# Output projection of an attention layer: single-precision matmuls replaced by three terms of halves, for all batches but the last

## The reference, cut to what matters

```python
    x = L0_attn_x
    xn = _layernorm(x, axis=-1)
    x = x + _L0_attn_ref(xn, ...) + _L0_ffn_ref(xn, ...)

    # the end of _L0_attn_ref, which the change is about
    y = jnp.einsum('bhqk,bhkd->bhqd', att, v)
    y = y.transpose(0, 2, 1, 3).reshape(Bx, Sx, Dx)
    return y @ W_proj + b_proj
```

## Time and profile before

| | us |
|---|---|
| median of three runs | 3735.48 |
| lowest and highest of them | 3733.85, 3745.34 |
| the profiled execution, its own time | 3740.65 |
| its span, first to last instruction | 3738.8 |
| TensorE (matmul) busy | 3660.0 (98%) |
| VectorE busy | 2638.5 (71%) |
| ScalarE busy | 1199.3 (32%) |
| GpSimd busy | 930.6 (25%) |

### The profile page before, as it was taken

One profiled execution on the slowest core, in us unless ns is written; L12 is line 12 of the kernel. 1 busy time (PEld: TensorE's weight loads), 2 busy tenths in 40 slices (PEclk: granted clock), 3 DMA queues, 4 the chain that ended last, 5 costly groups with the idle time before them and its releaser, 6 DMA issues.

```text
span 3738.8 us, 63849 instructions
## 1 busy us (share of the span) xinstructions
PE 3660.0 (98%) x21836; PEld 2699.9 (72%) x21836; DVE 2638.5 (71%) x3834; ACT 1199.3 (32%) x2313; POOL 930.6 (25%) x462
## 2 busy tenths in 40 slices
PE   8999999999999999999999999999999999999999
PEld 6657657657656566566565578888888888888887
DVE  6675766766766766766766667777777777777776
ACT  2542532533523524514414412222222222222222
POOL 0560741642632724615615500000000000000000
PEclk9999999999999999999999999999999999999999
DMA  6525435335336245254256331100111110011110
GB/s 199 124 72 178 109 101 175 77 123 165 80 120 173 63 144 155 58 185 123 73 179 172 119 122 34 34 31 28 34 34 34 34 32 31 30 34 34 34 34 28
DMA packets 180526, 337.02 MB, mean 90 GB/s; under 512 B 42688, under 2 KB 50368, under 8 KB 179392
## 3 DMA queue, kind: packets, MB, share of 16 engines
q1 hardware_dynamic: 156096, 280.47, 26.5%
q10 hardware_dynamic: 24192, 53.49, 4.2%
HBM read 213.92 MB, written 118.43 MB: 89 GB/s over the span
## 4 chain that ended last, share of the span: by engine, by line
PE 90%; issue 2%; DMA 2%; DVE 2%; POOL 2%; ACT 1%; SPq 0%; ACTq 0%; DVEq 0%; POOLq 0%
PE f_ps L1523 26%; PE ps_dense L1016 13%; PE f_ps_o L1535 13%; PE ps_st L1072 9%; PE ps_s L1041 5%; PE ps_y L1093 4%; PE ps_dense L1180 4%; PE ps_dense L1093 3%; PE ps_dense L1111 3%; PE ps_dense L1041 2%; PE f_ps L1515 1%; PE ps_st L1079 1%; DMA stack<-mr 1%; POOL stage L585 1%; PE ps_s L1046 1%
## 5 line engine op out<-in xcount | busy, mean ns | idle before, releaser
L1523 PE MATMUL f_ps<-wgu,xqt 128*128 128x512 f32 (+1 forms) x4608 | 992.9, 373 | 1.4 <-DVE xqt L1383 1.4
L1523 PEld LDWEIGHTS f_ps<-wgu,xqt 128*128 128x128 f32 x4608 | 842.4, 188 | 123.0 <-DVE xqt L1383 1.7
L933 ACT ACTIVATE pt<-ps_st 128x512 f32<-128x512 f32 (+3 forms) x1152 | 550.4, 526 | 540.4 <-PE ps_st L1072 354.8
L653 DVE TENSOR_REDUCE mx<-ps_s 128x1 f32<-128x640 f32 (+3 forms) x512 | 523.8, 1023 | 212.2 <-PE ps_s L1046 203.1
L585 POOL TENSOR_TENSOR stage<-stage,pt 128x1536 f32<-128x1536 f32 (+2 forms) x176 | 519.1, 2950 | 15.2
L1535 PE MATMUL f_ps_o<-wd,hqt 128*128 128x512 f32 x2112 | 513.4, 396 | 0.2 <-DVE hqt L1409 0.2
L583 POOL TENSOR_TENSOR stage<-pt 128x1792 f32<-128x1792 f32 x64 | 256.5, 4009 | 882.6 <-ACT pt L933 882.6
L1535 PEld LDWEIGHTS f_ps_o<-wd,hqt 128*128 128x128 f32 x2112 | 392.6, 189 | 79.5 <-DVE hqt L1409 0.6
L1016 PE MATMUL ps_dense<-arena,wa 128*128 128x512 f32 x1536 | 384.1, 399 | 11.1 <-DVE rob L701 6.2
L1016 PEld LDWEIGHTS ps_dense<-arena,wa 128*128 128x128 f32 x1536 | 281.1, 189 | 73.7 <-issue 10.8
L653 DVE TENSOR_REDUCE mx<-ps_dense 128x1 f32<-128x128 f32 (+3 forms) x424 | 204.4, 482 | 87.5 <-PE ps_dense L1046 78.1
(11 more groups left out here) (135 smaller groups left out, 4943.1 us busy)
## 6 DMA issues: line engine op xcount, KB each, us to landing
qk_scratch<-stage SPq DMA_DIRECT2D x128, 512.0 KB, 2.8
stack<-qk_scratch SPq DMA_DIRECT2D x192, 256.0 KB
arena<-qk_scratch SPq DMA_DIRECT2D x192, 256.0 KB
xs<-in_L_attn_x SPq DMA_DIRECT2D x64, 256.0 KB, 3.6
rob<-in_L_attn_x ACTq DMA_DIRECT2D x64, 256.0 KB, 2.8
acc_scratch<-rob ACTq DMA_DIRECT2D x64, 256.0 KB, 2.2
xt<-in_L_attn_x SPq DMA_DIRECT2D x64, 256.0 KB, 2.6
at<-acc_scratch SPq DMA_DIRECT2D x64, 256.0 KB, 2.6
```

The source lines that it names most:

```text
L653: nc.vector.tensor_reduce(mx[:, h * ST + q:h * ST + q + 1], scores_bank(p, n)[:, 0:(q + 1) * P], axis=AX.X, op=ALU.max, negate=True).then_ ...
L933: nc.scalar.activation(exps(kt)[:, h, q - kt * P:q - kt * P + n], ps_st[:, w % ST_RING, 0:n], ACT.Exp, scale=SCALE).then_inc(st_exp, 1)
L1523: last = nc.tensor.matmul(ps[:, SLOT[c], gu, 0:n].rearrange("p (j n) -> p j n", n=P), xqt[:, a, k], wgu[:, b, gu * FC + f // P:gu * FC + ( ...
```

## The change

For all batches but the last (`not final`) the output projection is made as the first stage is, in three terms of halves. The high half of `wp` is made by ScalarE and its low half by GpSimd, two pieces each, behind pair 5, in the place of stack 0, for each batch anew. The high half of `yt` is made by ScalarE in the place of stack 1 and its low half by GpSimd in place over `yt`: groups 0 and 1 behind pair 6, group 2 behind pair 7. Group 3 of tiles 0 and 1 stays whole; for the other six tiles ScalarE makes its high halves in two pieces (256 and 512 columns) and VectorE the low ones, between `low_of_x(0)` and `low_of_x(1)`. The fourth `high_of_x` comes behind them on ScalarE. Four semaphores are new.

```diff
+    yt_low = memory.over("yt_low", [P, G, S], F32R, "yt")
...
+    wp_halves = stack01[:, 0].rearrange("p a (c n) -> p (a c) n", n=D)
+    yt_high = stack01[:, 1]
+    WHOLE = 2
+    LAST_COLS = [slice((ST // 2 + WHOLE) * P, S), slice(0, S // 2)]
+    NHALVES = G - 1 + len(LAST_COLS)
...
+            def low_of_wp(i):
+                rows = slice(i * KC // 2, (i + 1) * KC // 2)
+                pool.wait_ge(p_hi, ONE + b * 2 + i + 1)
+                nc.gpsimd.tensor_tensor(wp_halves[:, KC + i * KC // 2:KC + (i + 1) * KC // 2], wp[:, rows],
+                                        wp_halves[:, rows].bitcast(F32), ALU.subtract).then_inc(p_lo, 1)
+
+            def low_of_y(g):
+                pool.wait_ge(y_hi, ONE + b * NHALVES + g + 1)
+                nc.gpsimd.tensor_tensor(yt_low[:, g], yt[:, g], yt_high[:, g].bitcast(F32),
+                                        ALU.subtract).then_inc(y_lo, 1)
...
                 for kt in SUM_ORDER[:summed(p)]:
                     sum_up(p, kt)
+                if not final and p == PAIRS - 3:
+                    for i in range(2):
+                        low_of_wp(i)
+                if not final and p == PAIRS - 2:
+                    for g in range(G - 2):
+                        low_of_y(g)
+                if not final and p == PAIRS - 1:
+                    low_of_y(G - 2)
...
             divide(PAIRS - 1)
             if not final:
-                for t in range(XR):
+                low_of_x(b + 1, 0)
+                for i, cols in enumerate(LAST_COLS):
+                    dve.wait_ge(y_hi, ONE + b * NHALVES + G + i)
+                    dve.wait_ge(y_lo, ONE + b * NHALVES + G - 1 + i)
+                    nc.vector.tensor_tensor(yt_low[:, G - 1, cols], yt[:, G - 1, cols],
+                                            yt_high[:, G - 1, cols].bitcast(F32), ALU.subtract).then_inc(y_lo, 1)
+                for t in range(1, XR):
                     low_of_x(b + 1, t)
...
+            def high_of_wp(i):
+                rows = slice(i * KC // 2, (i + 1) * KC // 2)
+                nc.scalar.activation(wp_halves[:, rows], wp[:, rows], ACT.Copy).then_inc(p_hi, 1)
+
+            def high_of_y(g):
+                act.wait_ge(y_div, ONE + b * PAIRS * 2 + (g + 1) * 4)
+                nc.scalar.activation(yt_high[:, g], yt[:, g], ACT.Copy).then_inc(y_hi, 1)
...
+                    if not final and p == PAIRS - 3 and kt >= ST - 3 and kt < ST - 1:
+                        high_of_wp(kt - ST + 3)
+                    if not final and p == PAIRS - 2 and kt >= ST - 3 and kt < ST - 1:
+                        high_of_y(kt - ST + 3)
 
             if final:
                 shared.abs_first(act)
+            else:
+                high_of_y(G - 2)
             act.wait_ge(den_full, ONE + b * PAIRS + PAIRS)
             for k in range(2):
                 load(k)
             if not final:
-                for t in range(XR):
+                for t in range(XR - 1):
                     high_of_x(b + 1, t)
+                act.wait_ge(y_div, ONE + b * PAIRS * 2 + PAIRS * 2)
+                for cols in LAST_COLS:
+                    nc.scalar.activation(yt_high[:, G - 1, cols], yt[:, G - 1, cols], ACT.Copy).then_inc(y_hi, 1)
+                high_of_x(b + 1, XR - 1)
...
             def output(k, groups):
-                t = OUT[k]
+                rows = slice(OUT[k] * P, (OUT[k] + 1) * P)
                 for g in groups:
-                    last = nc.tensor.matmul(bank("P", k), yt[:, g, t * P:(t + 1) * P], wp[:, g, :],
-                                            start=g == 0, stop=g == G - 1)
+                    terms = [(yt[:, g, rows], wp[:, g])]
+                    if not final and (g < G - 1 or k >= WHOLE):
+                        high, low = yt_high[:, g, rows], yt_low[:, g, rows]
+                        terms = [(high, wp_halves[:, g]), (high, wp_halves[:, KC + g]), (low, wp_halves[:, g])]
+                    for i, (left, right) in enumerate(terms):
+                        last = nc.tensor.matmul(bank("P", k), left, right, start=g == 0 and i == 0,
+                                                stop=g == G - 1 and i == len(terms) - 1)
...
             pe.wait_ge(den_copy, ONE + b * NDEN + NDEN)
+            if not final:
+                pe.wait_ge(p_lo, ONE + b * 2 + 2)
+                pe.wait_ge(y_lo, ONE + b * NHALVES + G - 1)
...
                     emptied("P", k)
+                    if not final and OUT[k] * P in [cols.start for cols in LAST_COLS]:
+
+                        pe.wait_ge(y_lo, ONE + b * NHALVES + G + [cols.start for cols in LAST_COLS].index(OUT[k] * P))
                     output(k, range(G))
```

More of the change, by code:

```diff
@@ L234, in attention @@
     y_div = sem("a_y_div")
+    y_hi, y_lo = sem("a_y_hi"), sem("a_y_lo")
+    p_hi, p_lo = sem("a_p_hi"), sem("a_p_lo")
     res_in = [sem(f"a_res_in{i}") for i in range(2)]
@@ L249, in attention @@
               v_done, *stack_in, s_full, s_max, m_full, m_hi, m_lo, m_in, st_full, st_exp, pv_done, summed_up, den_full,
-              den_copy, den_in, inverted, last_inverted, inv_out, inv_in, y_div, *res_in, o_res, o_sum, *o_out,
+              den_copy, den_in, inverted, last_inverted, inv_out, inv_in, y_div, y_hi, y_lo, p_hi, p_lo, *res_in, o_res, o_sum, *o_out,
               *q_in, q_chain, q_t, q_abs, q_d, q_q, q_full, q_hi, q_lo, *q_out]
@@ L263, in stack @@
         return stack01[:, s] if s < 2 else arena[:, s - 2]
+    wp_halves = stack01[:, 0].rearrange("p a (c n) -> p (a c) n", n=D)
[3 more added lines that the diff above has]
+    NHALVES = G - 1 + len(LAST_COLS)
+    assert HG == 4 and [OUT[k] for k in range(WHOLE)] == [ST // 2, ST // 2 + 1]
     def bank(kind, i):
```

## The result

Before 3736.42 us (3733.85 to 3745.34, 4 runs), after 3761.53 us (3757.78 to 3770.77, 4 runs), ratio 1.0067, 95% interval [1.0041, 1.0092]. The forecast was 3741 us with a range that ended at 3754. A second comparison gave 3762.1 (5 runs) against 3739.8 us (17 runs), ratio 1.0058 [1.0045, 1.0071]. The profiled execution of the changed kernel took 3770.77 us (span 3769.0, granted clock 0.990), the second one's span was 3757.3 us.

What follows compares the result with a forecast made beforehand. VectorE's fixed list of adds, then the last residual load, was taken to bound the projection, not matmuls. Front +0.6, tail -1.1 and pairs +1.3 gave +0.8 us per batch, +5.6 in seven: 3741 us, 8-in-10 range 3726 to 3754.

Steps and rivals of the forecast that it cites:

- the 2.5: Sign of being wrong: a batch more than 2.5 us longer (or more than 1.5 us shorter).
- Matmuls: Output projection: terms of 0.216 us replace whole products, saving 7.2 us of TensorE time per batch, 50 us in seven.
- Tail: Projection's adds 5 to 7: the last add comes 1.1 us sooner per batch on average, bounds 0.4 and 2.1.
- Front: Start of the projection: VectorE's two added subtractions cost 0.6 us per batch, bounds 0.3 and 1.0.
- TensorE's own front gains nothing: Before the first add: cheaper terms gain nothing, as the fourth `transpose_x` still waits for `low_of_x(0)`.
- Pair 5: ScalarE's copy before the third exponential of pair 5 delays TensorE's third part by 0.7 us.
- Pair 6: ScalarE's copy in pair 6 costs 1.05 us, of which 0.6 is left after TensorE's wait for GpSimd's sums.
- GpSimd: New subtractions behind pairs 5 to 7: pair 7's first sum 1.7 us late but covered; group 2 hidden by 1.5 us.
- C: Rival: GpSimd's sums in pair 7 end late and denominators wait: 3751 us, at worst 3758; chance 0.22 together with D.
- D: Rival: halves not ready, TensorE waits for `y_lo`, costing what passes 1.5 us; part of C, joint chance 0.22.
- A: Rival: the projection's tail pays in full, the last residual landing in 2.8 us: 3727 us, best 3725; chance 0.15.
- B: Rival: TensorE bounds the projection after all, 3 to 7 us per batch gained: 3715 to 3685 us; chance 0.05.

Runs made afterwards that it cites:

- terms only: Kernel before the change, with the 30 products in three terms from ready-made halves and all splitting and its waits left out (wrong results): 3741.0 us, ratio 1.0002.
- the copies behind: Changed kernel with ScalarE's four copies issued after the last exponentials of pairs 5 and 6 instead of between them: 3751.62 us, ratio 1.0026.
- filled: Changed kernel plus ten unused 512-column matmuls behind tile 7, where TensorE waits for the last add: 3755.67 us, ratio 1.0042.
- whole and behind: Changed kernel with ScalarE's copies after the exponentials of pairs 5 and 6, and the last group whole in all eight tiles: 3748.18 us, ratio 1.002.
- the last one: Changed kernel with copies after the exponentials, last group whole in all tiles, and ten unused matmuls behind tile 7: 3740.17 us, ratio 0.9998.
- QK0 early: Changed kernel with the next batch's first product waiting for the seventh add instead of the eighth: 3771.19 us, ratio 1.0078.

## Why the prediction was wrong

The sign of the sum was right, its size was not: +0.8 us per batch forecast, +3.1 to 3.5 measured, past the 2.5 that I had named as a sign of being wrong. Of the 2.3 us that are missing in the second profile the tail has 1.0, stage A, which had no term, 0.7, the front 0.3 and the pairs 0.3.

- **Matmuls.** That cheaper matmuls bring nothing was right, by the run with terms only. The saving itself was put too high: a term follows the one before at 0.227 us (0.216 forecast) and an instruction of a whole product at 0.43 (0.44), so 210 products save 37 us by these distances, and the view has 31, not 50.
- **Tail: this step failed.** "So it moves by ... 1.1 us on average" became 0.0 (G 22.55 and 22.46 against 22.55). I took the wait of the residual from the kernel before, 7.2 to 5.4 us after `add(5)`, as if it were a property of the load. But the residual of tile 5 came late as well: its load took 3.4 us in each of seven batches, beside a fetch of code, and 2.7 before without one (table above). So `add(5)` stood 1.05 us waiting for GpSimd and came 15.6 us after `add(0)`, not 14.8; with terms only, where this load takes 2.69, it came at 14.83, as forecast. The load of tile 7 hangs on that add, so it was issued 0.4 us later (in batch 0 at 289.61, that is 16.8 us after `add(0)`; before 16.5), not 0.4 us sooner, and the median of all residual loads rose from 2.8 to 3.4 us. With terms only the gain was 0.63, under the forecast too, since the load of tile 7 took 4.31 us in the mean and not 3.97. Making TensorE quicker in a stage that ends with a chain of add, store and load shortened only TensorE's part of it.
- **Front: mis-sized in two terms.** Forecast +0.6, measured +0.9. "TensorE's own front gains nothing" was wrong: it gained 0.56, as shown above. "Together 1.1 us" for the two subtractions holds only where GpSimd has not started first: in batch 1 of the changed kernel they took 0.42 and 0.69. In batch 0 they took 1.92 us, because the first began at 269.15, inside a row of GpSimd that ends at 269.99:

```profile
267.30 2.69 POOL L582 TENSOR_TENSOR rob<-rob,bp 128x512 f32<-128x512 f32 x2 [4.20 <-DMA rob<-in_L_attn_x]
```

  The Trainium skill, "SBUF — State Buffer" (the shared port pair as an exclusive lock), says that the two engines exclude each other for a whole instruction; the trace agrees, 1.92 us against 1.1 by size. I had cited that rule and then taken a value below its end; F is 8.44 in batch 1 and 9.04 to 9.47 in the others.
- **Pair 5.** +0.7 forecast, D +0.65 measured, and gone with the copies behind: right.
- **Pair 6.** +0.6 forecast. E is +0.3 in batches 2 to 5 (27.68 against 27.38) and +1.8 in the other three, where a stretch at the lower clock stands behind the wait for ScalarE's exponential, as in batch 0:

```profile
237.00:240.00 3.00, 2.69 (x20) 1.40 (x18) 2.59 (x9) 2.86 (x6) 2.92 (x2) 1.00 0.03 6
240.00:243.00 3.00, 2.40 (x18) 1.50 (x20) 1.27 (x7) 2.21 (x6) 2.92 (x2) 0.59 0.27 87
```

  The mean, +0.9, is not far from the forecast, but by luck, from two errors that pull against each other: the wait at the sums covered more than I allowed (+0.3 in place of +0.6), and the clock, 1.5 us for each such stretch, wasn't in the sum.
- **Stage A: a missing term.** Nothing in the sum was for what stands behind the last add. A rose by 0.8 us per batch, 5 us in all, by ScalarE's lateness at QK0's outcome (above). TensorE's longer wait for the last add, 18.3 in place of 6.2 us, was in my own numbers (tile 7's products ready 2.1 us before the add); I asked neither what an idle TensorE nor what a ScalarE with its issues crowded behind the last add does next.
- **The clock: a missing term, but not in A.** The stretches behind the last add cost nothing that can be seen: without them, filled, A is 80.42, with them 80.26. There TensorE is slow while it would else wait for ScalarE: its waits ahead of QKV's rows for a `stage` shrank from 4.9 to 2.7 us. Where TensorE is not waiting the clock costs: 1.5 us in pair 6. The Trainium skill, "TensorE: Matmul & The Clock Gate" (Part 1), has the clock at one of two levels, 1.2 and 2.4 GHz, by how busy the engine has been; the trace agrees, with 0.50 from 565.00 to 568.00 and 1.00 from 561.00 to 564.00, and the 0.63, 0.80 and 0.59 above are slices that hold some of both.
- **GpSimd (rivals C and D).** Not borne out. Pair 7's first sum started 13.38 us ahead of the last reciprocal, as before (13.37), waiting for ScalarE and not late for GpSimd's own work, and the third subtraction (L607, 260.74, 2.37 us) ended before the first early product at 264.74:

```profile
243.82 4.70 POOL L607 TENSOR_TENSOR yt_low<-yt,stack 128x1024 fp32r<-128x1024 f32 x2
...
250.26 4.01 POOL L595 TENSOR_TENSOR stage<-pt 128x1792 f32<-128x1792 f32 x1 [0.42 <-ACT pt L978]
...
260.74 2.37 POOL L607 TENSOR_TENSOR yt_low<-yt,stack 128x1024 fp32r<-128x1024 f32 x1 [2.12 <-ACT stack L950]
```

  The time, 3761.5, lay on C's side, but above even its dear end (3758), and not by its mechanism. A and B fell with the run of terms only.

Open: how much the place of the code alone is worth, since no run moves it by itself; and why A rose by more than ScalarE's lateness in four versions (terms only 1.05 against 0.79, whole and behind 1.2 against 0.86, the last one 1.93 against 1.21, QK0 early 2.44 against 0.67).

## What to carry to other kernels

When an engine is made quicker in a stage that another engine ends, ask two things: which chain ends it next, followed link by link from its first late link, and what the work that now comes closer together does to the next stage, because here ScalarE, with its issues crowded behind the last adds, reached the next batch 0.8 us later. Work put "beside" a stage must be placed by the queue it stands in: the same four copies cost ten microseconds ahead of three exponentials and 0.1 us per batch behind them. Before a gain of a few microseconds is put down to an added instruction, compare where code is fetched in both traces. Price a two-input operation on VectorE beside GpSimd at the blocked duration.

## What was not expected of the hardware

Ten discarded products of 512 columns (2.43 us) made the tuned version 8 us quicker (ratio 1.002 to 0.9998) and did nothing to the kernel before. They took the stretches at the lower clock away, and yet the gain lay elsewhere: the last residual's load landed sooner, 4.05 in place of 5.06 us, with fewer fetches of code beside it. A load of 256 KB took 2.7 us without such a fetch and 3.4 with one, in each of seven batches. Releasing a stage one add earlier gained nothing (1.0078 against 1.0058), since ScalarE reached the outcome only after 11.59 us of "issue", 3.9 of them in the branch of its loop.
